# Two expert loops on one core: the narrow product reads the resident weight table, the copy keeps the wide product's weights

## The reference

```python
# layer 0: each token uses its two best experts; F = 256
h = silu(x @ w_gate[e].T) * (x @ w_up[e].T)
y = h @ w_down[e].T                      # weighted by the gate of (token, e), summed over two e
# layer 1: each token uses its best expert; F = 512
h = relu(x @ w1[e] + b1[e])
y = h @ w2[e] + b2[e]
```

## Time and profile before

| | us |
|---|---|
| median of three runs | 1153.78 |
| profiled execution, first to last instruction | 1175.1 |
| layer 0's expert loop, first `turn` to last (72 slots) | 551.8 to 666.6 |
| layer 1's expert loop, first `turn` to last (40 slots) | 1044.9 to 1119.5 |
| TensorE busy over the span | 878.0 (75%) |
| VectorE busy over the span | 887.3 (76%) |
| ScalarE, GpSimd busy over the span | 630.2 (54%), 738.3 (63%) |

### The profile page before, as it was taken

How to read it: one execution, slowest core, us unless ns; L and a number is a source line. 1 busy time by engine, 2 the same in 40 slices (tenths; PEclk the granted TensorE clock), 3 DMA queues, 4 the chain that set the end, 5 groups by cost and what they waited for, 6 DMA issues and landing times. The chain is left out here.

```text
span 1175.1 us, 14982 instructions
## 1 busy us (share of the span) xinstructions
PE 878.0 (75%) x4244; PEld 565.5 (48%) x4244; DVE 887.3 (76%) x1790; ACT 630.2 (54%) x1401; POOL 738.3 (63%) x508
## 2 busy tenths in 40 slices
PE   7797769886987787753999736596987978349930
PEld 4243324334433433333999713264665767339920
DVE  4896999899979999966666555486896878465512
ACT  4787635874587465516343313656567684246710
POOL 0898799989988999702666376355433443037646
PEclk8999989998999898865999967598989977569975
DMA  6644445455544554340233312111101020142323
GB/s 185 184 131 131 125 147 166 137 157 160 162 131 143 164 164 156 113 164 13 71 85 87 72 50 68 45 34 50 45 2 64 28 74 19 54 165 73 71 63 98
DMA packets 90905, 118.95 MB, mean 101 GB/s; under 512 B 12508, under 2 KB 48804, under 8 KB 90696
## 3 DMA queue, kind: packets, MB, share of 16 engines
q1 hardware_dynamic: 84168, 104.34, 28.7%
q0 software_dynamic: 6656, 13.64, 5.0%
HBM read 103.70 MB, written 14.25 MB: 100 GB/s over the span
## 5 line engine op out<-in xcount | busy, mean ns | idle before, releaser
L687 POOL TENSOR_TENSOR ma_bu<-ma_u,ma_row_b 128x1024 f32<-128x1024 f32 x128 | 300.7, 2377 | 15.6 <-DVE ma_u L898 8.0
L416 PE MATMUL y_ps<-ma_h,ident 128*128 128x512 f32 x512 | 254.1, 635 | 27.4 <-POOL ma_h L697 23.1
L1215 POOL DMA_INDIRECT s_rows<-xs,take x112 | 128.9, 1151 | 162.3 <-POOLq L951 105.6
L563 ACT ACTIVATE decay_ps<-ma_delta,negA 128x512 f32<-128x512 f32 x256 | 172.5, 686 | 85.8 <-DVE ma_h L790 82.9
L416 PEld LDWEIGHTS y_ps<-ma_h,ident 128*128 128x128 f32 x512 | 100.4, 204 | 156.1 <-issue 111.1
L1568 POOL TENSOR_TENSOR mi_dec<-mi_dec,mi_gm 128x512 f32<-128x512 f32 x32 | 40.7, 1272 | 135.0 <-DVE mi_gm L2033 111.5
L1232 PE MATMUL s_up_ps<-s_xt,s_w 128*128 128x128 f32 x896 | 122.6, 282 | 1.2 <-ACT s_xt L1259 1.2
L780 DVE TENSOR_TENSOR_SCAN decay_ps<-decay_ps,ma_carry,ma_bu 128x512 f32<-128x512 f32 x88 | 110.1, 1271 | 12.6 <-issue 9.7
L790 DVE TENSOR_TENSOR ma_h<-decay_ps,ma_row_c 128x512 f32<-128x512 f32 x176 | 116.9, 665 | 0.0
L1232 PEld LDWEIGHTS s_up_ps<-s_xt,s_w 128*128 128x128 f32 x896 | 113.2, 198 | 1.6 <-DVE s_w L1291 1.0
L697 POOL TENSOR_TENSOR ma_h<-ma_h,ma_row_c 128x1024 f32<-128x1024 f32 x40 | 97.1, 2428 | 17.4 <-DVE ma_h L780 15.6
(11 more groups left out here) (323 smaller groups left out, 1766.0 us busy)
## 6 DMA issues: line engine op xcount, KB each, us to landing
ma_row_b<-bc_rows SPq DMA_DIRECT2D x128, 256.0 KB, 3.6
ma_row_c<-bc_rows SPq DMA_DIRECT2D x128, 256.0 KB, 3.3
mi_cs<-cs_rows SPq DMA_DIRECT2D x32, 256.0 KB
ys<-s_outs SPq DMA_DIRECT2D x28, 256.0 KB
w<-in_experts SPq DMA_DIRECT2D x1, 4112.0 KB, 14.9
w<-in_experts SPq DMA_DIRECT2D x1, 3072.0 KB, 10.3
xs<-rows SPq DMA_DIRECT2D x4, 512.0 KB, 3.4
out<-X SPq DMA_DIRECT2D x8, 256.0 KB
```

Of the source, the lines that this page charges most:

```text
L416: mm = pe.matmul(y_ps[:, j, :], m.ident[:], h[g % HS][:, j, :], start=False, stop=True, skip_group_check=True)
L563: act.activation(decay[s % DS][:], delta[b % 2][:, j, col(c)], ACT.Exp, scale=m.negA0[:, j, n:n + 1]).then_inc(decay_done, 1)
L687: pool.tensor_tensor(bu[g % BUS][:], u[b % 2][:, :, col(c)], both(row_b[g % BS]), ALU.mult).then_inc(bu_done, 1)
L1215: pool.indirect_dma_start(rows[s % ROWS][:], None, m.xs[layer], bass.IndirectOffsetOnAxis(ap=m.take[:, s:s + 1], axis=0)).then_inc(fetched ...
```

## The change

The rows of the resident table are laid out so that the narrow product's weights come last in either layer. VectorE copies only the front part, `KEPT[layer]` numbers wide: 512 in place of 768 in layer 0, and 644 in place of 1156 in layer 1 (wide weights, first bias, second bias). TensorE loads the owners into registers of its own every eight slots, and each matmul of the narrow product takes its moving operand from `m.w[layer]` at an address made from a register. Layer 1's table is loaded by three transfers in place of two.

```diff
-WIDTH = (3 * F0, 2 * F1 + F1 // P + P)
-LATE = (80, 112)
+WIDTH = (3 * F0, F1 + F1 // P + P + F1)
+KEPT = (2 * F0, F1 + F1 // P + P)
+LATE = (80, 128)
...
-                own = WIDTH[1] - P
-                sp.dma_start(m.w[1][:, :, 0:own], a["experts1"]).then_inc(m.late, 16)
-                sp.dma_start(m.w[1][:, :, own:], a["L1_ffn_b2"].partition_broadcast(P)).then_inc(m.late, 16)
+                own = KEPT[1] - P
+                sp.dma_start(m.w[1][:, :, 0:own], a["experts1"][:, :, 0:own]).then_inc(m.late, 16)
+                sp.dma_start(m.w[1][:, :, KEPT[1]:], a["experts1"][:, :, own:]).then_inc(m.late, 16)
+                sp.dma_start(m.w[1][:, :, own:KEPT[1]], a["L1_ffn_b2"].partition_broadcast(P)).then_inc(m.late, 16)
...
-    width = WIDTH[layer]
+    width = KEPT[layer]
...
         def _(pe):
+            registers = [pe.alloc_register(f"{tag}pe_owner{i}") for i in range(READ)]
...
             def narrow(s):
+                if s % READ == 0:
+                    pe.load(registers, m.owner[0:1, s:s + READ])
+                expert = pe.snap(registers[s % READ], min_val=0, max_val=NE - 1)
                 pe.wait_ge(ht_done, base + s + 1)
                 if s >= 2:
                     pe.wait_ge(out_read, base + s - 1)
                 for f in range(FB):
                     mm = pe.matmul(out_ps[s % 2][:, 0:P], ht[s % HS][:, f * P:(f + 1) * P],
-                                   w[s % WS][:, UP + f * P:UP + (f + 1) * P], start=(f == 0), stop=(f == FB - 1))
+                                   m.w[layer][:, bass.ds(expert, 1), width + f * P:width + (f + 1) * P].rearrange(
+                                       "p o f -> p (o f)"), start=(f == 0), stop=(f == FB - 1))
                 mm.then_inc(out_done, 1)
...
-                                             ACT.Relu, bias=w[s % WS][:, 2 * F1 + f:2 * F1 + f + 1])
+                                             ACT.Relu, bias=w[s % WS][:, F1 + f:F1 + f + 1])
...
                 expert = dve.snap(registers[s % READ], min_val=0, max_val=NE - 1)
-                dve.tensor_copy(w[s % WS][:], m.w[layer][:, bass.ds(expert, 1), :].rearrange("p o f -> p (o f)")
-                                ).then_inc(copied, 1)
+                dve.tensor_copy(w[s % WS][:], m.w[layer][:, bass.ds(expert, 1), 0:width].rearrange(
+                    "p o f -> p (o f)")).then_inc(copied, 1)
...
-                    dve.tensor_tensor(dst, out_ps[s % 2][:, 0:P], w[s % WS][:, 2 * F1 + FB:2 * F1 + FB + P], ALU.add
+                    dve.tensor_tensor(dst, out_ps[s % 2][:, 0:P], w[s % WS][:, F1 + FB:F1 + FB + P], ALU.add
...
-        return np.ascontiguousarray(np.concatenate([by_row("L1_ffn_w1"), by_row("L1_ffn_w2"), b1], axis=2))
+        return np.ascontiguousarray(np.concatenate([by_row("L1_ffn_w1"), b1, by_row("L1_ffn_w2")], axis=2))
```

## The result

The kernel after takes 1161.05 us (median of 18 runs) beside 1154.27 us for the kernel before in the same series (18 runs). The ratio is 1.0043, with a 95% interval of 1.0029 to 1.0058: 5.0 us slower, between 3.3 and 6.7. That is less than the half per cent named in the prediction. The forecast was 1159.5 us, 5.7 above before. The two medians lie 6.8 us apart, just beyond the upper end of the interval; what follows goes by the ratio.

The account below looks back on a forecast made before the run. TensorE's pairs were taken to bound layer 1, pairs and a two-slot loop together layer 0. Terms 5.0 + 0 + 0.4 + 0 + 0.3 - 0 = 5.7 us on 1153.8 gave 1159.5 us, range 1152 to 1171.

Parts of the forecast that it names:

- The bound: Layer 1: TensorE's 17 pairs, 1.90 us a slot; layer 0: 13 pairs and a two-slot loop through four engines, both 1.45.
- the main term: TensorE's register work in layer 0's loop: 0.15 us per two slots, 5.0 us over 67 slots.
- the first rival: Register addresses are free on TensorE, decoded like fixed ones: 1.4 us in all, 1155 us; chance 0.31.
- its own test: Layer 0, narrow product's weights to next `widen`: grows from 0.55 to about 0.7 us; unchanged speaks for free register addresses.
- The register operations: TensorE, one per narrow product (144 and 160), near 0.07 us each.
- The register load: TensorE loads eight owners every eight slots, 14 loads of some 0.6 us, hidden: 0 us.
- Its rival: TensorE's load takes 1.6 us, its excess added once per eight slots of layer 0: 4.5 us more, 1164; chance 0.06.
- VectorE's copies: Shorter copies, 0.46 and 0.52 us, free 18.1 us of VectorE but gain 0; at most 1.8 us.
- Layer 1 and its table: Layer 1's loop work hidden, 0 us; SyncE's three transfers in place of two show 0.3 us.
- the last narrow products: The last narrow product of either layer has no cover: 0.4 us for both layers.
- The late completions: Some fifteen late layer 0 slots cost 10.2 us; rival: shorter VectorE copies remove two thirds, 1148 us; chance 0.10.

Follow-up runs that it names:

- before's second profile: The kernel before, unchanged, profiled once more: span 1156.3 us, layer 0's 67 slots 97.37 us.
- the wait on the matmul: Kernel after with the wait for `out_read` put on the first narrow matmul, behind its address's register operation: 67 slots 97.38 us, ratio 1.0016 to before.
- the move behind the waits: Kernel after with the register move of the owner put behind both waits of the narrow product: 67 slots 102.71 us, ratio 1.0051 to before.
- the waits swapped: Kernel after with the event taking `ht_done` and the register operation `out_read`: 67 slots 98.48 us, ratio 1.0016 to before.

## Why the prediction was right, and where it wasn't

**The bound.** Right. Layer 1 is bound by its pairs (64.46, to 0.01, in before's second profile and in every version), layer 0 by two limits that meet: opening one of them alone gains 0.28 us, and adding 0.141 to the loop costs half of it per slot.

**The size of the main term.** 0.15 us on the loop was forecast, 5.0 us in all; 0.141 and 4.9 were measured. **Its place was wrong,** and so was its reason. The prediction split the 0.15 into 0.02 ahead of the narrow product and 0.13 behind its start, at 0.07 for each matmul with a register address. Behind, nothing changed: from narrow's weights to the next `widen` it is 0.55 us in after as in the earlier trace rows, and the new work disappeared in the slack. The prediction put 0.56 us from the event for `out_read` to `turn`'s; measured it is 0.106 + 0.138 + 0.124 = 0.37, event and two register operations. Register addresses are free, as the first rival held. From the second register operation to the next event the sequencer takes 0.124 us, as long as the 0.125 from event to event before. The estimate that a register address sends each matmul through firmware, at the 62 ns which the Trainium skill ("TensorE: Matmul & The Clock Gate", section "Step-by-step: what each phase is for") gives for a matmul without the decoder, is not borne out: no matmul with a register address shows a price of its own here.

Ahead of the narrow product, the step that failed is the sentence "the wait itself now sits on a register operation of 67 in place of 51 ns, 0.02 more". It took the register operation to replace the event. Two waits stand there: the event keeps `out_read` and the register operation gets `ht_done`, so the two come one after the other. The step as the prediction described it, one wait on a register operation in place of an event, measured 0.034 us; the event that stays ahead of it adds 0.107, its place in the row and not its 51 ns. So 0.141 stood where 0.02 was put, and 0 where 0.13 was put: two mis-sized terms that nearly cancelled, by luck. What the prediction named as its own test, the distance from narrow's weights to the next `widen` growing to 0.7, came out unchanged; by its own words that spoke for the rival at 1155 us, and the runs were 5 us above before all the same. The right total is no proof of the step.

**The register operations.** One per narrow product was right (304 = 144 + 160); they take 46 to 60 ns, not 67. The move per slot, 29 ns each, was missing in the prediction; it stands ahead of the waits and costs nothing.

**The register load.** Right: 14 loads of 0.59 us, hidden. Its rival, an estimate of 1.6 us from the Trainium skill ("Runtime: NRT & Kernel Launch", section "Instruction fetch mechanics", about 200 ns per register), is refuted for this load, which reads the owners from SBUF, by 594 ns for eight registers; no run here loads registers from other memory.

**VectorE's copies.** Worth 0, as forecast; the copies took 0.43 and 0.49 us where 0.46 and 0.52 were worked out. In the regular slots of the earlier trace rows the copy isn't in the loop, and whole rows gave the same length.

**Layer 1 and its table.** 0 for the loop was right. For the table 0.3 us was forecast; in after's profile SyncE's wait ends 0.9 us before the block does and nothing shows, in two other profiles 0.1 and 0.2 us do. For the last narrow products 0.4 us was forecast in both layers together: from layer 0's last `turn` to the end of its block it is 8.28 us in after and 7.99 in before's second profile, 0.3 more, and in layer 1 8.64 in both. Together with the loop that makes 5.2 us, where the runs have 5.0 (3.3 to 6.7).

**The late completions.** The prediction read the earlier trace rows as a feature of the kernel, and gave a chance to their going away. They were a feature of one execution, whose span of 1175.1 us stood 21 us above the median: 10.0 us of that were in layer 0's loop (107.38 against 97.37), and 10.1 between the last `turn` of layer 0 and the first of layer 1 (378.2 against 368.1 us). Adding the sum to the median and not to that span was what kept the number right. Why completions come late in some executions stays open; one such slot of 2.57 us turned up in the kernel with the change in layer 0 alone, and slots of 1.78 and 1.76 us with the wait on the matmul and the move behind the waits.

## What to carry to other kernels

When an instruction waits for several things, list every sequencer instruction between the last wait and the work, and charge each its place in the row (here 0.11 to 0.14 us on TensorE) and not its own duration; then put the last wait on the work itself, behind the first address's arithmetic, which here gave back the whole loss of the loop. Before costing an edit on an engine that isn't the bound, open the loop that ties it to the bound (one more PSUM tile): it shows at once what there is to gain, here 0.28 us of 97. And profile the kernel before twice when its profiled span stands well above the median of its runs.

## What the hardware did that was not expected

- Where TensorE's sequencer doesn't wait, it starts events, moves and register operations 0.09 to 0.15 us apart, although these last 29 to 68 ns: 0.087 from the move to the event with the waits swapped, 0.106 in after from the event for `out_read` to the register operation, 0.138 from the first register operation to the second with a product between them, 0.147 with the move behind the waits. An event whose waits have long passed costs the same (0.104 us).
- The moving operand's address from a register cost nothing: layer 0's 67 slots took 97.38 us with a register operation for each product and the wait on the matmul, 97.39 at a fixed address.
- A register move and an address calculation that stand side by side became one register operation, of 68 ns in place of 60.
- TensorE's busy time doesn't show this loss. In after's layer 0 it reads 102.27 of 102.27 us, as the modelled ends of its matmuls cover the waits (one of 372 ns stands where the others have 275); only the weight loads leave 1.8 us idle of the 4.9 lost.
